# Cross-attention with a routed feed-forward: the attention stage in groups of four pairs

## The reference

```
xn = layernorm(x)
q, k, v = xn Wq' + bq, ctx Wk' + bk, ctx Wv' + bv      16 heads of 8 numbers
x1 = x + softmax(q k' / sqrt(8), masked) v Wo' + bo      within each sequence
z = layernorm(x1); probs = softmax(z Wr + br)            8 experts
e = argmax(probs); gate = max(probs)
y = relu((layernorm(z) ln_g + ln_b) W1[e] + b1[e]) W2[e] + b2[e]
out = x1 + gate y
```

## Time and profile before

| what | value |
|---|---|
| runs | 393.29, 390.35, 392.4 us; median 392.4 |
| profiled execution | 394.74 us |
| its span | 393.0 us |
| mean granted TensorE clock | 0.85 |
| busy: PE, PEld | 303.1 us (77%), 240.2 us (61%) |
| busy: DVE | 304.9 us (78%) |
| busy: ACT, POOL | 202.0 us (51%), 163.5 us (42%) |
| moved by DMA | 36.31 MB, mean 92 GB/s |

### The profile page before, as it was taken

One profiled execution on the slowest core, in us unless ns is written; L12 is line 12 of the kernel. 1 busy time (PEld: TensorE's weight loads), 2 busy tenths in 40 slices (PEclk: granted clock), 3 DMA queues, 4 the chain that ended last, 5 costly groups with the idle time before them and its releaser, 6 DMA issues.

```text
span 393.0 us, 10023 instructions
## 1 busy us (share of the span) xinstructions
PE 303.1 (77%) x3066; PEld 240.2 (61%) x3066; DVE 304.9 (78%) x1159; ACT 202.0 (51%) x548; POOL 163.5 (42%) x220
## 2 busy tenths in 40 slices
PE   0449888788998878877798988963079898978990
PEld 0327656556875655654585776762078887867880
DVE  1247899999989999999999999756747776767771
ACT  1127666466456555646546465511056666656650
POOL 3314445455435545545544543333104443434442
PEclk9999989978568997999968595555569999999997
DMA  5955543234325333424324324000011112112110
GB/s 127 416 132 145 147 137 104 84 111 136 87 85 155 93 90 107 136 84 139 110 85 133 89 84 125 10 14 14 16 42 43 54 54 61 42 50 64 54 32 3
DMA packets 58228, 36.31 MB, mean 92 GB/s; under 512 B 5295, under 2 KB 56116, under 8 KB 58176
## 3 DMA queue, kind: packets, MB, share of 16 engines
q1 hardware_dynamic: 54592, 31.30, 27.5%
q0 software_dynamic: 2272, 4.27, 3.3%
q10 hardware_dynamic: 1312, 0.11, 0.5%
HBM read 14.03 MB, written 22.09 MB: 92 GB/s over the span
## 4 chain that ended last, share of the span: by engine, by line
issue 37%; DVE 31%; POOL 15%; DMA 6%; PE 5%; DVEq 2%; ACTq 1%; POOLq 1%; SPq 0%; ACT 0%
POOL rows_dram L355 5%; DVE Pr L539 3%; DVE mx L535 3%; POOL rs L333 3%; POOL row L343 3%; DMA out<-ot,G 3%; DVE hT L660 3%; DVE xt L500 3%; DVE xh L648 3%; DVE ot L669 2%; POOL xb L338 2%; POOL Kb L348 2%; DMA G<-rows_dram 2%; DVE yb L667 2%; DMA Wr<-in_wr 1%
## 5 line engine op out<-in xcount | busy, mean ns | idle before, releaser
L366 POOL DMA_INDIRECT out<-ot,G x39 | 39.8, 1020 | 67.8 <-DVE ot L669 66.7
L343 POOL TENSOR_TENSOR row<-ve,half 128x2 f32<-128x2 f32 x32 | 24.7, 771 | 103.1 <-DVE ve L589 103.1
L413 ACT ACTIVATE Pr<-Pr,rowany 128x1024 f32<-128x1024 f32 x32 | 36.7, 1148 | 59.8 <-DVE Pr L539 59.8
L706 PE MATMUL ps<-ident,Pr 128*128 128x128 f32 x256 | 51.2, 335 | 0.1
L396 ACT ACTIVATE PT<-ps 128x512 f32<-128x512 f32 x64 | 38.2, 597 | 18.4 <-PE ps L706 17.6
L706 PEld LDWEIGHTS ps<-ident,Pr 128*128 128x128 f32 x256 | 37.0, 173 | 16.8 <-issue 9.1
L796 PE MATMUL ps<-xg,WR 128*128 128x128 f32 x312 | 45.5, 291 | 0.0
L752 PE MATMUL ps<-VB,PT 128*64 128x18 f32 x1024 | 42.1, 228 | 0.3 <-ACT GT L403 0.3
L535 DVE TENSOR_REDUCE mx<-ps 128x16 f32<-128x1024 f32 x32 | 38.9, 1216 | 3.3 <-PE ps L695 3.3
L807 PE MATMUL ps<-WR,hT 128*128 128x128 f32 x312 | 41.2, 276 | 0.0
L796 PEld LDWEIGHTS ps<-xg,WR 128*128 128x128 f32 x312 | 39.5, 199 | 1.4
(11 more groups left out here) (113 smaller groups left out, 633.8 us busy)
## 6 DMA issues: line engine op xcount, KB each, us to landing
rows_dram<-empty SPq DMA_DIRECT2D x32, 528.0 KB, 4.4
WA<-in_wpk SPq DMA_DIRECT2D x8, 578.0 KB, 9.2
G<-rows_dram SPq DMA_DIRECT2D x39, 66.0 KB, 1.9
X<-in_x SPq DMA_DIRECT2D x32, 64.0 KB, 4.1
C<-in_ctxT SPq DMA_DIRECT2D x32, 64.0 KB, 1.8
Cv<-in_ctxT SPq DMA_DIRECT2D x32, 64.0 KB, 2.0
out<-ot,G POOLq DMA_INDIRECT x39, 2.3
rows_dram<-row,posi POOLq DMA_INDIRECT x32, 2.5
```

Source lines behind the costliest of these rows:

```text
L366: g.indirect_dma_start(out=out, out_offset=bass.IndirectOffsetOnAxis(ap=G[:, q, D + 2:D + 3].bitcast(I32), axis=0), in_=ot[:, q, :], in_of ...
L413: a.activation(Pr[:, q, :], Pr[:, q, :], ACT.Exp, scale=rowany[:, 0:1]).then_inc(s_p, 1)
L706: last = nc.tensor.transpose(ps[:, 4 + m, 128 * j:128 * j + 128], Pr[:, q, 128 * (4 * m + j):128 * (4 * m + j) + 128], ident[:])
```

## The change

The attention stage is written anew; the expert stage is the same but for column numbers, as a row has 134 floats (rstd, second power, two shifts, token number, gate) instead of 132.

- **Groups and units.** The projections work on groups of `GP = 4` pairs. What follows the attention of a pair works on units: seven of four pairs, then one of 2, 1 and 1. A step is still one pair; `unit_at(i, lag)` gives the unit whose last pair is `lag` steps back, `group_at(i, lead)` the group whose first pair is `lead` steps ahead. The steps run from -8 to `NP + 10`. The drain after the last pair has lags up to 10.
- **Loads.** `X` and `C` have a place for everything. SP issues 16 loads of 256 KB, with four weight loads after the first two, then four fills, the expert weights, and the other 28 fills one behind another. `Cv` is gone.
- **Scores** have two sets of two banks, by turns. `pen` is two matmuls of 512 columns on two row groups. The score matmuls go in two halves of four with a semaphore between them, and between the halves stands one of K, transposes of xn, Q, V.
- **Projections**: K and Q are one matmul of 512 columns for a group, V is sixteen of 64 columns, placed so that ScalarE needs two copies for a group instead of four for a pair.
- **ScalarE** normalises `xn` and `xt` (scale and bias from columns; the bias is a new shift that DVE computes for a whole group). It copies `xnT`, `xtT` and `OT` apart, 512 columns each.
- **DVE** does the residual add, the logits, the one-hot and the places for a unit at once. The sum of the gate's exponentials is a DVE reduction instead of ScalarE's accumulator.
- **GpSimd** takes the powers of a unit in one operation, up to eight columns. `xb` is made for a unit. `Kb` has three buffers. Scatters are still one for each pair, of a full unit's four one in a step, of the small units all at once.
- **Banks** 4 to 7 are each shared by several uses; `filled` and `freed` are one semaphore pair for a bank, and `fill_order` gives the number of each use.

```diff
+UNITS = [(GP * g, GP) for g in range(NG - 1)] + [(NP - 4, 2), (NP - 2, 1), (NP - 1, 1)]
...
+            load(0)
+            for W, w in ((Wk, wkT), (Wq, wqT), (Wv, wvT), (Wo, woT)):
+                sp.dma_start(W[:], w).then_inc(s_w[0], 16)
+            for g in range(1, NG):
+                load(g)
...
+            for j in range(4):
+                fill(j)
...
+            for j in range(4, NP):
+                fill(j)
...  (GpSimd)
+                if (t := unit_at(i, 5)):
+                    u, first, n = t
+                    pool.wait_ge(s_ve2, 2 * u + 2)
+                    g.tensor_tensor(out=row[:, u % UR, 0:n, D:D + 2], in0=ve2[:, u % 2, 0:n, :],
+                                    in1=half[:, None, :].to_broadcast([P, n, 2]), op=ALU.pow).then_inc(s_rs2, 1)
...
+                if 0 <= i + 2 < NP:
+                    p = i + 2
+                    pool.wait_ge(freed[7], nth("k", p // GP))
+                    wait(pool, s_s, p - 2)
+                    g.tensor_tensor(out=Kb[:, p % 3, :, :], ...).then_inc(s_kb, 1)
...  (ScalarE)
+                if (t := unit_at(i, 6)):
+                    u, first, n = t
+                    act.wait_ge(s_nm2, u + 1)
+                    for k in range(n):
+                        a.activation(xt[:, k, :], row[:, u % UR, k, 0:D], ACT.Identity, bias=row[:, u % UR, k, D + 2:D + 3],
+                                     scale=row[:, u % UR, k, D:D + 1]).then_inc(s_xt, 1)
...  (TensorE)
+            def scores(i, half_of):
+                q, c = i // GP % 2, P * (i % GP)
+                for j in (half_of, 2 + half_of):
+                    for b in range(2):
+                        last = mm(ps[64 * b:64 * b + 64, 2 * (i % 2) + j // 2, 256 * half_of:256 * half_of + 256],
+                                  QT[32 * j:32 * j + 32, q, c + 64 * b:c + 64 * b + 64],
+                                  Kb[32 * j:32 * j + 32, i % 3, :, 64 * b:64 * b + 64], ...)
+                return last
+            for i in range(FIRST, LAST):
+                if 0 <= i < NP:
+                    pe.wait_ge(freed[7], nth("q", i // GP))
+                    pe.wait_ge(s_kb, i + 1)
+                    wait(pe, s_sub, i - 1)
+                    for m in range(2):
+                        mm(ps[:, 2 * (i % 2) + m, :], eye2[64 * m:64 * m + 64]..., pen[64 * m:64 * m + 64]..., ...)
+                    scores(i, 0).then_inc(s_sh, 1)
+                if (gr := group_at(i, 4)) is not None:      # K, one matmul of 512
+                if (gr := group_at(i, 3)) is not None:      # four transposes of xn
+                if (gr := group_at(i, 2)) is not None:      # Q, one matmul of 512
+                if (gr := group_at(i, 1)) is not None:      # V
+                    for b in range(2 * GP):
+                        for h2 in range(2):
+                            last = mm(ps[64 * h2:64 * h2 + 64, 7, 64 * b:64 * b + 64], C[:, ... 64 columns],
+                                      Wv[:].rearrange("p (j t d) -> p j t d", t=2, d=DK)[:, :, h2, :], ...)
+                if 0 <= i < NP:
+                    pe.wait_ge(s_sh, i + 1)
+                    scores(i, 1).then_inc(s_s, 1)
+                # then, in this order: transposes of Pr (i - 1), PV (i - 2),
+                # units: xt transposes (lag 6), On transposes (3), Wo (4), Wr (7), ranks (9)
```

More of the change, by code:

```diff
@@ L205, in build, with nth, unit_of, done_pairs @@
         block = ctx.enter_context(nc.Block())
[L207 to L211, removed]
+        def nth(*key):
+            return fills[key]
+        def unit_of(p):
+            return next(u for u, (first, n) in enumerate(UNITS) if first <= p < first + n)
+        def done_pairs(u):
+            return UNITS[u][0] + UNITS[u][1]
+        def rows_out(u):
+            return 16 * sum(UNITS[w][1] for w in range(u % UR, u + 1, UR))
         def w1_of(s, c):
@@ L359, in _, with scatter @@
-            for j in range(-3, A1):
-                step(j // 2, j % 2)
+            def scatter(p):
+                u = unit_of(p)
+                r, k = u % UR, p - UNITS[u][0]
+                pool.wait_ge(s_fill[p % 4], 16 * (p // 4 + 1))
+                settle(last_row)
+                g.indirect_dma_start(out=rows, out_offset=bass.IndirectOffsetOnAxis(ap=posi[:, r, k:k + 1], axis=0),
+                                     in_=row[:, r, k, :], in_offset=None, bounds_check=last_row,
+                                     oob_is_err=False).then_inc(r_out[r], 16)
@@ L768, in step @@
-                if (t := pair(h, u, 0)):
-                    p, n, q = t
-                    pe.wait_ge(cv_in[q], 16 * (n + 1))
-                    last = mm(psV, Cv[:, q, :], Wv[:], start=True, stop=True)
-                if last is not None:
-                    last.then_inc(s_pj, 1)
-            for j in range(-2, A1):
-                step(j // 2, j % 2)
-            pe.wait_ge(s_rt, 7 * NP)
-            pe.wait_ge(s_v, 4 * NP)
-            mm(ps[0:1, 7, 0:E], ones[:, 0:1], seen[:, NP % 2, :], start=True, stop=True).then_inc(s_tot, 1)
+                    last.then_inc(filled[6], 1)
@@ new lines, in _ @@
+                if (t := unit_at(i, 4)):
+                    u, first, n = t
+                    pe.wait_ge(freed[5], nth("onT", u))
+                    wait(pe, freed[4], nth("o", u) - 1)
+                    for k in range(n):
+                        last = mm(ps[:, 4, P * k:P * k + P], OT[:, P * k:P * k + P], Wo[:], start=True, stop=True)
+                    last.then_inc(filled[4], 1)
+                if (t := unit_at(i, 7)):
+                    u, first, n = t
+                    pe.wait_ge(freed[5], nth("xtT", u))
+                    wait(pe, freed[4], nth("l", u) - 1)
+                    for k in range(n):
+                        last = mm(psL[:, E * k:E * k + E], xtT[:, P * k:P * k + P], Wr[:], start=True, stop=True)
+                    last.then_inc(filled[4], 1)
```

808 lines of the change are left out of this document (409 added, 399 removed).

## The result

The changed kernel takes 414.4 us (median of 4 runs, 408.75 to 416.44) against 392.7 us before: a ratio of 1.052, 95% interval 1.040 to 1.063. It is slower; the forecast was 355 and faster. A ratio leaves out runs more than 1.5% above the fastest of their kernel; where the clock differs from run to run that drops many, so I give medians of all runs beside it, and no ratio where too few are left.

The account below looks back on a forecast made before the run. The prediction took VectorE to bound the kernel before and TensorE after. Head 22.7, four steps at 5.3, 27 at 6.61, drain 17, slot table 7.2 and expert stage 109.2 gave 355.8, hence 355 us; range 335 to 377.

Parts of the forecast that it names:

- TensorE becomes the bound: Attention steps: TensorE needs 5.6 us per pair at full clock; step by step 25.1 a group, 6.28 a pair.
- I take 0.15: Steady pairs: share of time at half clock 0.15, against 0.3 before, making 6.28 us a pair 6.61.
- 0.9 of waiting for `xt`: TensorE's group work in the step with xt transposes: 0.9 us waiting for ScalarE's xt, within 2.35.
- 1.2 more for the slow power: Once per group: the slow GpSimd power delays xt and Kb alike, 1.2 us added to 23.9, giving 25.1.
- The price of half clock itself: Attention steps at half clock: 5.6 us scaled like 5.29 to 8.98, giving 9.4 us a pair.
- four pairs run at 5.3 us: First four attention steps have no older work behind them: 5.3 us each.
- Rival (d): TensorE caught at 1.2 GHz in 27 steady pairs, 3.1 us each; slower than before from share 0.64; chance 0.07.
- Drain: Last maximum to the totals: one single-pair unit's chain 15.7 us, with queues 17 instead of 27.6.
- the scatters covered by the slot table: At the end eight scatters of 1.06 us finish about 5 us after the totals, covered by the slot table's 7.2.
- Head: Start to first maximum: loads, projections and scores in series, 22.7 us instead of 25.2.
- Expert stage: After the first gather: left alone except for row width, 109.2 us as before.
- Rival (b): Attention steps: queue lockstep and TensorE array-form switches add 10 to 16 us with a queue wait: 366 to 372; chance 0.20.

Follow-up runs that it names:

- the wait filled: Changed kernel plus five idle matmuls in front of TensorE's wait for xt of each full unit: 363.58 us, ratio 0.920 to the changed kernel.
- experiments 1 and 6: 1: changed kernel, xt transposes two steps later 379.65 us, or wait filled with idle matmuls 363.58 us. 6: other aids kept, xt wait put back, 407.32 us.
- experiment 7: Changed kernel with the last four pairs as one unit: 409.97 us. Faster variant with three idle matmuls in each drain step: 367.72 us.
- Scatters at once: Four scatters of the last full unit issued in one step, plus twelve idle matmuls at the start, on the variant with softmax waits filled: 357.19 us.
- a warm head: Twelve idle matmuls at the start, first on the changed kernel with the xt wait filled: 366.07 us against 363.58 without.
- experiment 5: Changed kernel, xt later, Kb first, idle matmuls before the exponential wait: 357.88 us; plus warm head and scatters at once 357.19, repeated 360.9; three early waits filled 356.1.
- experiment 1: Changed kernel with xt transposes and all behind them two steps later: 379.65 us; or five idle matmuls in front of the wait: 363.58 us.
- the first run of experiment 4: Changed kernel with xt transposes two steps later and, on GpSimd, Kb of pair i + 2 ahead of power and scatters: 362.91 us, ratio 0.917.
- the units of four: Changed kernel with the last four pairs as one unit of four instead of units of 2, 1 and 1: 409.97 us.

## Why the prediction was wrong

- **"TensorE becomes the bound"** was right, and so was its size at full clock: 24.4 us a group with the wait filled (the idle matmuls stand where the wait stood), against 25.1. The sum hides errors that cancel in part: V with sixteen packed matmuls took 1.08 (forecast 1.7), K and Q 1.06 each (0.88), the power of eight columns 1.65 (2.0). VectorE was busy for 3.9 us a pair (4.7).
- **The step that failed is the clock**: "I take 0.15" for the share at 1.2 GHz, with the reason that gaps of 2.1 us a step "most go". Over the same 27 pairs it was 0.61 (0.70 from the first fall on). The reason counted the gaps together and did not ask how they lie. Before, three waits of 0.4 to 0.6 us stood spread over each step (the earlier trace rows shows one); after, one wait comes in every fourth step, 2.63 us long when TensorE is at full clock for it the first time. The working of the forecast had this very gap: 0.9 of waiting for `xt`, 1.2 more for the slow power, 2.1 in all. I priced it at its own length, 2.1 us a group, and not at what it does to the clock, which experiments 1 and 6 put at 46 to 51 us in all. The price of half clock itself, 9.4 us a pair, was near: the first four slow intervals are 9.85 in the mean.
- **What the table hides.** The intervals missed by only 25.4 us, though the clock cost 45.8 (225.1 against 179.3 with the wait filled). Of the difference 8.9 are the forecast's own allowance of 0.15, and 11.5 are luck: at full clock the sum has 190.8 for what took 179.3. It let four pairs run at 5.3 us before the full 6.28; in fact the first nine intervals took 4.7 in the mean. The other 31 us of the miss are head, drain and expert stage.
- **Rival (d)** had the mechanism and the place, TensorE caught at 1.2 GHz in the steady pairs, at a chance of 0.07. Its point for "slower" was a share of 0.64; measured were 0.61, and the intervals alone gave back the gain and no more. That the kernel is clearly slower than before comes from the ends.
- **Drain**, "17 instead of 27.6" to the totals: it took 33.9 (254.6 to 288.6), the second large miss. The term was the chain of one unit, with TensorE's product already at half clock. The queues carry four units there and each step hands a small piece from engine to engine: that is my reading of the timelines, not tested. The clock can be at most some 11 us of it (experiment 7). Behind it the forecast had the scatters covered by the slot table; the last was issued at 295.1, 0.6 us after the table was ready, and its landing held the first gather for 5.2 us, where before it was 1.2. Scatters at once took 2 us of this back.
- **Head**, 22.7 forecast, 29.5 measured. The first K, Q and V ran at half speed, in the changed kernel's chain of waits:

```profile
13.67 2.06 PE ps L749 x2
19.91 2.09 PE ps L758 x2
22.76 1.98 PE ps L763 x32
```

  I had taken their prices from full clock; a warm head brought the first maximum 3.3 to 5.3 us forward (experiment 5). The profile shows 1.00 in this stretch, before the first change of the clock that it records; the durations show 1.2 GHz. So the clock row's start is not to be read alone.
- **Expert stage**: 113.0 for 109.2 with the same code. Over the profiled runs here it was 106 to 114 us. I did not test why.
- Rival (b), array switches: no drain is seen. From the start of the first half of the scores to that of Q it is 0.59 us in the run with the filled wait (75.24 to 75.83), less than the scores' record of 0.66; and as long from the second half to the probability transposes (76.89 to 77.48). The Trainium skill's rule in TensorEngine Tiling (Array Packing), cited in the prediction, would have added a wait there, which this trace does not show.
- Small slips in the recorded sums: 5.6 scaled like 5.29 to 8.98 is 9.5, not 9.4; the once-a-group terms of TensorE add up to 7.6, not 7.7; the head's terms as listed to 22.4, not 22.7. None matters here.

What brings the clock back within the kernel's own steps (3 us at times, 44 at others) stays open. So does what else trips it. In the profiles of the changed kernel and its variants it fell 63 times between 20 us and the last maximum, and at 19 of these no gap of 0.4 us or more lies within the 6 us before. So a gap like that of 2.6 us is enough, but it isn't the only cause. Open too is the spread of 20 us and more between runs of the faster variants.

## What to carry to other kernels

When a change makes TensorE the bound, its gaps can get a second price, the clock: look first for the longest single wait in its new queue, not for the sum of waits, and move the consumer a step or two later, or fill the wait, before anything else is tuned. Then read the new trace, as the next wait may take its place (experiment 1), and don't expect every fall of the clock to go. While another engine is the bound, as VectorE was here before, the same clock may cost nothing and a clock row with dips says little. And price the ends of a pipeline by themselves: here they, not the middle, made the kernel slower than before. A queue order written out by hand should be read with the producer's whole chain beside it (power, shift, four normalisations), as one late piece blocks every piece behind it.

## What the runs showed of the hardware

- In the profiles of the changed kernel and its variants, from 20 us to the last maximum, TensorE had 27 gaps of 1.05 to 2.64 us at full clock, and the clock fell in each of them or within 2.2 us behind it. Shorter ones did not always do it: it fell right behind a gap of 0.68 us in the changed kernel and held through four of them in the run with the filled wait; it held through gaps of 0.82 and 0.66 us in one step, twice, in the first run of experiment 4; two gaps of 0.8 us at the head came with a fall in the five profiles with a warm head that had them both, and with none in the run with the filled wait and that of the units of four. 19 of 63 falls had no gap of 0.4 us near.
- TensorE busy without a break at half clock did not bring the clock back for 36 us in the changed kernel (80 to 116 us); with ten matmul records of 256 float32 columns in a row it was back within 3.7 to 5.9 us of their start, seven of seven times. The kernel's own steps at times did as well (3.4 us) and at times needed 44.
- Before the first change that a profile records, the clock row says 1.00 whatever the matmuls' durations say: 2.06 us for the first K, 1.06 at full clock.
- A GpSimd power costs 0.57, 0.80 and 1.65 us for one, two and eight columns of 128 partitions.
- ScalarE's scale and bias from columns, 128 x 128 from SBUF, took 0.48 us a record, four in a row 1.65.
